# Cross-attention: two heads' row maxima turned by one transposition and carried to the queries' rows by SyncE's queue

## The chip, the cores and the metric

The kernel runs on one core of one Trainium2 chip. The metric is the device time of one execution in microseconds (us), as the median of several runs. The core's engines are TensorE (PE in the profile, with PEld for its weight loads), VectorE (DVE), ScalarE (ACT), GpSimd (POOL) and SyncE (SP), which here only issues transfers (DMAs). Each works through its own instruction stream in order, and they meet at semaphores.

## The reference

A decoder layer on `x` (16 x 224 x 512, float32): causal self-attention with rotary positions, cross-attention over a context of 750 positions, and a mixture-of-experts feed-forward part, each behind a layer norm and with a residual. The change lies in the cross-attention:

```python
q = (x @ Wq).reshape(B, N, HEADS, hd).transpose(0, 2, 1, 3)         # B 16, N 224, HEADS 16, hd 32
k = (context @ Wk).reshape(B, M, HEADS, hd).transpose(0, 2, 1, 3)   # M 750
v = (context @ Wv).reshape(B, M, HEADS, hd).transpose(0, 2, 1, 3)
scores = jnp.einsum('bhid,bhjd->bhij', q, k) * scale
scores = jnp.where(context_mask[:, None, None, :], scores, max_neg)
attn = jax.nn.softmax(scores, axis=-1)
out = jnp.einsum('bhij,bhjd->bhid', attn, v)
out = out.transpose(0, 2, 1, 3).reshape(B, N, DIM)
return out @ Wo
```

## The kernel before

The three parts of the layer run one after the other; the cross-attention is the function `cross_attention`. It loops over 16 batches `b`, and in each over four groups `g` of four heads `j`. With `t = 4 * b + g` a group is numbered through the whole stage. Batches 2 to 14 are iterations of a hardware loop; the first two and the last are written out.

**Scores twice.** For each head TensorE first forms the scores with the queries as rows (`scores`, two halves `h` of 112 queries), and VectorE takes their row maximum (`maximum`) into `mx`, 112 queries on partitions, [head, half] along the free side. One group later TensorE forms them again with the keys as rows (`shifted`, three units of 2 x 125 keys), this time with the maximum already taken off, so that ScalarE can go straight to the exponential (`exps`). For that the operands are stacked. `q_st` holds per head 32 rows of high parts, 32 again, 32 of low parts, then row 96 (ones) and rows 97 and 98: the negated maximum of each query, split into a high and a low part. `k_st` holds the keys' parts in its first 96 rows, the mask in row 96 and ones in rows 97 and 98. `scores` uses rows 0 to 96, `shifted` rows 0 to 98.

**How the maximum gets there.** `turn_max(u, t, i)` handles two heads (`i` = 0: heads 0 and 1, `i` = 1: heads 2 and 3). For each of their four columns of `mx` (two heads, two halves) it transposes the column, broadcast to 128 columns, so that the maxima of 112 queries stand along the free side of every partition of a PSUM bank `pj`. `high_max` on ScalarE writes rows 96 to 98 of `q_st` from the same rows of that bank, and `low_max` on VectorE corrects them with a per-row factor `less`, so that row 96 is 1, row 97 the high and row 98 the low part. TensorE waits for `low_max` (`done(...)`, the semaphore `pj_free`) before the first `shifted` of these heads.

**The order.** All engines follow a schedule written by hand. For each head of a group TensorE's stream holds `scores` of half 0, `shifted` of the same head of the group before (two units), `first_gap`, the third unit, `scores` of half 1 and `second_gap`; after four heads come the `values` of the group before. The gaps hold the projections of coming keys, queries and values, each into one of three banks `pj`, taken in turn and named by `UNITS`. Two kinds of these units are maximum turns. `M0_g` (`i` = 0 of group g) is turned in the first gap of head 3 and needed at head 0 of the next group. `M1_g` (`i` = 1 of the group before g) is turned in the second gap of head 0 of group g and needed at head 2 of the same group.

**SyncE's queue** issues all transfers in one order: `place_k` (copies of the projected key parts into four slots of `k_st`, 3 or 4 transfers a head, 16 for groups 0 and 1, 12 for groups 2 and 3), `place_q` (12 transfers for half of the heads), the loads of context and mask (`load_ctx`), of `x` and of the residual, and the stores. `place_k` waits until both halves of the keys are split (units `K..0`, `K..1`, VectorE's `low_k`) and, per head, until `shifted` is through with the slot.

Of the kernel before, what the change touches and what calls it, by code (L numbers as in the profile page):

```python
# [6 lines left out]
F32 = mybir.dt.float32  # L7
# [9 lines left out]
P = 128  # L17
# [807 lines left out]
def cross_attention(nc, x1, x1n, ctx, cmask, w_o, router_w, cst, x2, rows_w, logits, op):  # L825

    with ExitStack() as outer:
# [9 lines left out]
        with ExitStack() as c:  # L837
# [11 lines left out]
            mx = sb(c, "x_mx", [HT, 4, 2])  # L849
            less = sb(c, "x_less", [P, 1])  # L850
            pt = [op.pt[0], sb(c, "x_pt1", [KR, 3, 2 * T]), op.pt[2], op.pt[3]]
# [10 lines left out]

            gate, filled, zeroed, stored, rw_turned, rw_out, wo_loaded = (
                sem("x_" + n) for n in ("gate", "filled", "zeroed", "stored", "rw_turned", "rw_out", "wo_loaded"))
            x_loaded, c_loaded, m_loaded, xres_loaded = op.x_loaded, op.c_loaded, op.m_loaded, op.xres_loaded
# [24 lines left out]
            def k_mult(g):  # L890

                return 16 * (4 if g < 2 else 3)

            def placed(b, g):
# [11 lines left out]
            with nc.Block() as block:  # L906
                @block.sync
                def _(sp):
# [29 lines left out]
                    def place_k(t, b, g, units):  # L938
# [5 lines left out]
                        if below(t, 1):  # L944
                            sp.wait_ge(zeroed, 1)
                        for j in range(4):
# [12 lines left out]
                    def place_q(b, half, units):  # L959
# [5 lines left out]
                        for j in range(4):  # L965
                            rows = slice(32 * j, 32 * j + 32)
                            for s, p in enumerate((0, 0, 1)):
                                sp.dma_start(q_st[32 * s:32 * s + 32, 8 * half + j:8 * half + 8:4, :].bitcast(F32),
                                             qT[p][rows, 2 * half:2 * half + 2, :].bitcast(F32)).then_inc(q_placed[half], 16)

                    load_x(1, unit_of(-1, "X1"))
                    sp.dma_start(wo[:], w_o.rearrange("(k p) n -> p k n", p=P)).then_inc(wo_loaded, 16)
# [5 lines left out]
                    def body(b, first, last, more):  # L978
                        t = 4 * b
                        if not last:  # L980
                            load_ctx(b + 1)
                        place_k(t + 1, b, 1, [unit_of(b, "K10"), unit_of(b, "K11")])
                        place_q(b, 1, [unit_of(b, "Q2"), unit_of(b, "Q3")])
                        if not below(b, 2):
                            load_res(b - 1)
                            store_rows(b - 2)
                        place_k(t + 2, b, 2, [unit_of(b, "K20"), unit_of(b, "K21")])
                        if more:
                            load_x(b + 2, unit_of(b, "X1"))
                        place_k(t + 3, b, 3, [unit_of(b, "K30"), unit_of(b, "K31")])  # L990
                        if not first:
                            store(b - 1, unit_of(b, "O1"))
                        if not last:
                            place_q(b + 1, 0, [unit_of(b, "Q0"), unit_of(b, "Q1")])
                        if not last:
                            place_k(t + 4, b + 1, 0, [unit_of(b, "K00"), unit_of(b, "K01")])

                    body(0, True, False, True)
# [16 lines left out]
                def _(pool):  # L1015

                    fills = [(ones[:], 1.0), (less[:], -1.0), (less[96:97, :], 0.0)]
                    fills += [(k[96:99, :].bitcast(F32), 1.0) for k in k_st]
                    for n, (f, value) in enumerate(fills):
                        pool.memset(f, value).then_inc(filled, 1)  # L1020
                        pool.wait_ge(filled, n + 1)
                    pool.nop().then_inc(zeroed, 1)

# [45 lines left out]
                def _(pe):  # L1069
# [143 lines left out]
                    pe.wait_ge(rw_out, 1)  # L1213
                    pe.wait_ge(zeroed, 1)
                    pe.wait_ge(wo_loaded, 16)

                    def body(b, first, last):
# [79 lines left out]
                        for g in range(4):  # L1297
# [3 lines left out]
                            for j in range(4):  # L1301
                                pe.wait_ge(k_placed[j], placed(b, g))
                                scores(n, g, j, 0)
                                if prev:
                                    if j == 0:
                                        done(U(f"M0_{gp}") if g else unit_of(b - 1, "M0_3"))
                                    elif j == 2:
                                        done(U(f"M1_{g}"))
                                    shifted(n - 1, gp, j, (0, 1))
                                first_gap(g, j)  # L1310
                                if prev:
                                    shifted(n - 1, gp, j, (2,))
                                scores(n, g, j, 1)
                                second_gap(g, j)
# [13 lines left out]
                    n, last = 4 * B, lambda name: unit_of(B - 1, name)  # L1328
                    done(last("M0_3"))
                    shifted(n - 1, 3, 0, range(3))  # L1330
                    turn_max(last("M1_4"), n - 1, 1)
# [4 lines left out]
                    done(last("M1_4"))  # L1336
                    shifted(n - 1, 3, 2, range(3))
# [18 lines left out]
                def _(act):  # L1356
# [104 lines left out]
                    def body(b, first, last):  # L1461
# [6 lines left out]
                        def first_gap(g, j):  # L1468
# [13 lines left out]
                            elif j == 3:  # L1482
                                high_max(U(f"M0_{g}"), g, 0)
                                if g == 0 and not last:
                                    high_x(U("X0"), 0)
                                elif g == 1 and old:
                                    out_rows(U("N1"), 1)
                                elif g == 2 and not last:
                                    high_ctx(U("C01"), 0, 1)

                        def second_gap(g, j):
                            gp, prev = (g + 3) % 4, not (first and g == 0)
                            if j == 0:
# [7 lines left out]
                                if prev:  # L1501
                                    high_max(U(f"M1_{g}"), gp, 1)
                            elif j == 1:
# [50 lines left out]
                    n = 4 * B  # L1554
                    exps(n - 1, 0, range(3))
                    high_max(unit_of(B - 1, "M1_4"), 3, 1)
                    for j in range(1, 4):
                        exps(n - 1, j, range(3))
# [8 lines left out]
                def _(dve):  # L1567
# [97 lines left out]
                    def body(b, first, last):  # L1665
# [6 lines left out]
                        def first_gap(g, j):  # L1672
                            n, prev, pprev, gp = t + g, not (first and g == 0), not (first and g < 2), (g + 3) % 4
                            if j == 0:
# [4 lines left out]
                            elif j == 1:  # L1679
                                if prev:  # L1680
                                    low_max(U(f"M1_{g}"), 2 * n, gp, 1)
                            elif j == 2:
                                if pprev:
                                    invert(n - 2, 0)
                            else:
# [4 lines left out]
                                if g == 2 and not last:  # L1690
                                    low_ctx(b, 2, 0)
                                low_max(U(f"M0_{g}"), 2 * n + 1, g, 0)

# [67 lines left out]

                    n = 4 * B
                    root(RLN_STEPS * (B - 1))
# [4 lines left out]
                    low_max(unit_of(B - 1, "M1_4"), 2 * n, 3, 1)  # L1768
                    dve.wait_ge(exp_done, 3 * 4 * n)
# [728 lines left out]
```

## Time and profile before

| | |
|---|---|
| median of 3 runs | 3782.72 us (3779.25 to 3786.2) |
| span of the profiled execution (first to last instruction) | 3781.0 us |
| TensorE busy | 3636.5 us, 96% |
| VectorE busy | 2363.4 us, 63% |
| ScalarE busy | 1731.8 us, 46% |
| GpSimd busy | 1298.8 us, 34% |
| maximum turns (512 transpositions), busy | 71.1 us |

The span is what the profile gives as the time of its execution; the runs' median is 1.7 us above it. The cross-attention takes from about 1075 to 2470 us of the span. The durations of TensorE's matmuls overlap, since they are pipelined: how long a part of its stream takes is read from one start to the next, not from the durations.

### The profile page before, as it was taken

The numbers are of one execution on the slowest core, as the hardware profiler recorded it, in microseconds if no ns is written. First come the engines' busy times: TensorE is split into PE (matmuls) and PEld (weight loads), VectorE is DVE, ScalarE is ACT, GpSimd is POOL, SyncE is SP. The second block draws the span as 40 slices with busy tenths as digits, with TensorE's granted clock in tenths as the row PEclk, the third lists the DMA queues.
The fourth block names the chain that finished last, engine by engine and source line by source line (L and its number), as shares of the span: only waits on it lengthen the run. The fifth ranks groups of instructions, "written<-read, shape, count | busy, mean of one in ns | idle before, by whom it ended". The sixth has DMA issues, their size and how long they took to land. (4 is left out here: it accounts for less than half of the span.)

```text
span 3781.0 us, 84211 instructions
## 1 busy us (share of the span) xinstructions
PE 3636.5 (96%) x28244; PEld 3136.9 (83%) x28244; DVE 2363.4 (63%) x5547; ACT 1731.8 (46%) x4277; POOL 1298.8 (34%) x1385
## 2 busy tenths in 40 slices
PE   7999999999979999999999999849999999999999
PEld 6888888888868888888888888639999899989998
DVE  6788888888856666666666666576434434334343
ACT  4555555555535555555555555413333333333332
POOL 1333333333316556666556566510101101011010
PEclk9999999999979999999999999869999999999999
DMA  4222222222243343444434443223424334243232
GB/s 125 59 54 63 54 63 54 63 54 63 50 138 100 104 111 105 107 116 107 123 96 111 106 107 97 66 69 93 123 84 123 101 99 123 84 121 121 86 108 69
DMA packets 315057, 349.72 MB, mean 92 GB/s; under 512 B 45308, under 2 KB 232036, under 8 KB 314884
## 3 DMA queue, kind: packets, MB, share of 16 engines
q1 hardware_dynamic: 305796, 318.26, 30.7%
q0 software_dynamic: 9088, 29.17, 2.5%
q8 instruction: 106, 1.74, 0.2%
q14 instruction: 67, 0.55, 0.0%
HBM read 183.23 MB, written 38.91 MB: 59 GB/s over the span
## 5 line engine op out<-in xcount | busy, mean ns | idle before, releaser
L1605 DVE TENSOR_REDUCE x_mx<-x_psS 112x1 f32<-112x752 f32 x512 | 479.8, 937 | 380.1 <-PE x_psS L1158 376.7
L2401 DVE TENSOR_TENSOR hid<-e_psU,act_g 128x280 f32<-128x280 f32 x256 | 115.2, 450 | 626.1 <-PE e_psU L34 616.0
L1440 ACT ACTIVATE x_pt<-x_psE 125x448 f32<-125x448 f32 x768 | 389.5, 542 | 231.3 <-PE x_psE L1170 221.9
L1029 POOL TENSOR_TENSOR part<-x_pt 125x448 f32<-125x448 f32 x255 | 291.7, 1144 | 507.3 <-ACT x_pt L1440 498.5
L2027 POOL DMA_INDIRECT out<-ex_y,sidx x40 | 39.8, 994 | 1014.7 <-DVE ex_y L2435 1007.0
L611 POOL TENSOR_TENSOR qks<-qks,cos 128x448 f32<-128x448 f32 x128 | 147.6, 1153 | 677.7 <-DMA qks<-qk 677.7
L1158 PE MATMUL x_psS<-k_st,q_st 97*112 97x376 f32 x1024 | 287.4, 362 | 23.4 <-DMA k_st<-mk 15.5
L32 PE MATMUL e_psG<-ex_hi,g_hi 128*128 128x280 f32 x1024 | 303.8, 297 | 4.3 <-DVE ex_lo L2394 2.2
L32 PE MATMUL pj<-xT_hi,win_hi 128*128 128x224 f32 x1024 | 302.8, 296 | 1.4 <-DVE xT_lo L651 1.3
L1031 POOL TENSOR_TENSOR part<-part,x_pt 125x448 f32<-125x448 f32 x255 | 291.8, 1144 | 20.0
L32 PE MATMUL e_psU<-ex_hi,u_hi 128*128 128x280 f32 x1024 | 298.1, 291 | 0.3 <-DVE hid L2401 0.3
L34 PE MATMUL e_psG<-ex_hi,g_lo 128*128 128x280 f32 x1024 | 298.3, 291 | 0.0
L2186 ACT ACTIVATE act_g<-e_psG 128x280 f32<-128x280 f32 x256 | 103.7, 405 | 423.6 <-PE e_psG L34 417.0
L34 PE MATMUL e_psU<-ex_hi,u_lo 128*128 128x280 f32 x1024 | 297.6, 291 | 0.0
L33 PE MATMUL e_psG<-ex_lo,g_hi 128*128 128x280 f32 x1024 | 297.0, 290 | 0.0
L33 PE MATMUL e_psU<-ex_lo,u_hi 128*128 128x280 f32 x1024 | 297.0, 290 | 0.0
L34 PE MATMUL pj<-xT_hi,win_lo 128*128 128x224 f32 x1024 | 282.3, 276 | 0.0
L33 PE MATMUL pj<-xT_lo,win_hi 128*128 128x224 f32 x1024 | 281.6, 275 | 0.0
L1170 PE MATMUL x_psE<-q_st,k_st 99*125 99x224 f32 x1536 | 262.9, 280 | 6.4 <-ACT x_pt L1440 4.1
L1170 PEld LDWEIGHTS x_psE<-q_st,k_st 99*125 99x125 f32 x1536 | 236.0, 190 | 15.8 <-ACT x_pt L1440 11.3
L2190 ACT ACTIVATE hid_hi<-hid 128x280 fp32r<-128x280 f32 (+1 forms) x256 | 107.1, 419 | 288.3 <-DVE hid L2401 288.3
L674 DVE CUSTOM_DVE_ANT_0 pr<-psS,mask 112x112 f32<-112x112 f32 (+1 forms) x512 | 139.4, 329 | 128.1 <-issue 67.5
(301 smaller groups left out, 10880.3 us busy)
## 6 DMA issues: line engine op xcount, KB each, us to landing
k_st<-kT SPq DMA_DIRECT2D x768, 93.8 KB, 2.2
raw_g<-in_L_ffn_wg SPq DMA_DIRECT2D x128, 256.0 KB, 2.8
raw_u<-in_L_ffn_wu SPq DMA_DIRECT2D x128, 256.0 KB, 2.8
raw_d<-in_L_ffn_wd SPq DMA_DIRECT2D x128, 256.0 KB, 3.0
qks<-qk SPq DMA_DIRECT2D x512, 56.0 KB, 2.0
q_st<-qT SPq DMA_DIRECT2D x384, 56.0 KB, 2.0
ctxt<-in_ctx SPq DMA_DIRECT2D x16, 1125.0 KB
xt<-in_x SPq DMA_DIRECT2D x16, 448.0 KB, 3.7
```

The lines of the kernel that those rows point to most:

```text
L32: pe.matmul(out, lh, rh, start=first, stop=False)
L33: pe.matmul(out, lh, rl, start=False, stop=False)
L34: return pe.matmul(out, ll, rh, start=False, stop=last)
L611: pool.tensor_tensor(qks[i][:], qks[i][:], cos[:].unsqueeze(1).to_broadcast((P, 2, T)), ALU.mult)
L674: m = dve.tensor_tensor_reduce(pr[par][:, hd, to:to + n], psS[hd][0:HT, to:to + n], mask[:, h, 0:n], -SD ** -0.5, -NEG, ALU.add, ALU.min, ...
L1029: pool.tensor_tensor(part[:], pt[j][:, 0, :], pt[j][:, 1, :], ALU.add).then_inc(parted, 1)
L1031: pool.tensor_tensor(part[:], part[:], pt[j][:, 2, :], ALU.add).then_inc(parted, 1)
L1158: m = pe.matmul(psS[0:HT, s, 0:376], q_st[0:97, head, h * HT:(h + 1) * HT], k_st[4 * (g % 2) + j][0:97, SHALF[s]], start=True, stop=True)
L1170: m = pe.matmul(psE[(j + i) % 2][0:KR, s * T:(s + 1) * T], k_st[4 * (g % 2) + j][0:99, r * KR:(r + 1) * KR], q_st[0:99, 4 * g + j, :], sta ...
L1440: act.activation(pt[j][:, i, :], psE[(j + i) % 2][0:KR, 0:2 * T], ACT.Exp, scale=XD ** -0.5).then_inc(exp_done, 1)
L1605: dve.tensor_reduce(mx[:, j, h:h + 1], psS[0:HT, :, 0:376], AX.XY, ALU.max).then_inc(s_taken, 1)
L2401: dve.tensor_tensor(h[ring][:, halves[s]], psU[:, 0:CH], act_g[i][:, halves[s]], ALU.mult).then_inc(S["mul"], 1)
```

## The change

`turn_max` makes one transposition of the four columns together: `mx[:, 2i:2i+2, :]` is a weight of four columns, and the maxima come out on four partitions of the bank, 112 queries along the free side. ScalarE writes the negated high parts to `m_row[:, 0, :]`, VectorE the low parts to `m_row[:, 1, :]` (4 x 112 each). `place_max` on SyncE's queue then copies `m_row[:, 0, :]` to row 97 and `m_row[:, 1, :]` to row 98 of `q_st` for the two heads, two transfers that count up a new semaphore `m_placed`. TensorE waits for that semaphore, and ScalarE, before it overwrites `m_row`, for the copies before. Eight calls of `place_max` a batch stand in SyncE's order between the others. Row 96 of `q_st` is written once ahead of the stage and stays.

```diff
-            less = sb(c, "x_less", [P, 1])
+            m_row = sb(c, "m_row", [4, 2, HT], F32R)
...
+            def max_placed(t, i):
+
+                return 64 * t + 32 * i + 32
+
+            fills = [ones[:]] + [k[96:99, :].bitcast(F32) for k in k_st]
...
+                    def place_max(u, g, i):
+
+                        hold(sp, gate, pj_free[u.bank], u.after)
+                        head = 4 * g + 2 * i
+                        for r in range(2):
+                            sp.dma_start(q_st[97 + r:98 + r, head:head + 2, :].rearrange("p j (h t) -> p (j h) t", h=2).bitcast(F32),
+                                         m_row[:, r, :].bitcast(F32)).then_inc(m_placed, 16)
+
...
                         if not last:
                             load_ctx(b + 1)
+                        if not first:
+                            place_max(unit_of(b, "M1_0"), 3, 1)
                         place_k(t + 1, b, 1, [unit_of(b, "K10"), unit_of(b, "K11")])
+                        place_max(unit_of(b, "M0_0"), 0, 0)
                         place_q(b, 1, [unit_of(b, "Q2"), unit_of(b, "Q3")])
                         if not below(b, 2):
                             load_res(b - 1)
                             store_rows(b - 2)
+                        place_max(unit_of(b, "M1_1"), 0, 1)
                         place_k(t + 2, b, 2, [unit_of(b, "K20"), unit_of(b, "K21")])
+                        place_max(unit_of(b, "M0_1"), 1, 0)
                         if more:
                             load_x(b + 2, unit_of(b, "X1"))
+                        place_max(unit_of(b, "M1_2"), 1, 1)
                         place_k(t + 3, b, 3, [unit_of(b, "K30"), unit_of(b, "K31")])
+                        place_max(unit_of(b, "M0_2"), 2, 0)
                         if not first:
                             store(b - 1, unit_of(b, "O1"))
                         if not last:
                             place_q(b + 1, 0, [unit_of(b, "Q0"), unit_of(b, "Q1")])
+                        place_max(unit_of(b, "M1_3"), 2, 1)
                         if not last:
                             place_k(t + 4, b + 1, 0, [unit_of(b, "K00"), unit_of(b, "K01")])
+                        place_max(unit_of(b, "M0_3"), 3, 0)
...
+                    place_max(unit_of(B - 1, "M1_4"), 3, 1)
...
-                    fills = [(ones[:], 1.0), (less[:], -1.0), (less[96:97, :], 0.0)]
-                    fills += [(k[96:99, :].bitcast(F32), 1.0) for k in k_st]
...
                         pe.wait_ge(s_taken, 8 * t + 4 * i + 4)
                         o = bank(u)
-                        for n in range(4):
-                            m = pe.transpose(o[:, n * HT:(n + 1) * HT], mx[:, 2 * i + n // 2, n % 2:n % 2 + 1].to_broadcast((HT, P)),
-                                             ident[0:HT, 0:HT])
-                        m.then_inc(pj_full, 1)
+                        pe.transpose(o[0:4, 0:HT], mx[:, 2 * i:2 * i + 2, :].rearrange("p j h -> p (j h)"),
+                                     ident[0:HT, 0:HT]).then_inc(pj_full, 1)
...
                                 if prev:
-                                    if j == 0:
-                                        done(U(f"M0_{gp}") if g else unit_of(b - 1, "M0_3"))
-                                    elif j == 2:
-                                        done(U(f"M1_{g}"))
+                                    if j in (0, 2):
+                                        pe.wait_ge(m_placed, max_placed(n - 1, j // 2))
                                     shifted(n - 1, gp, j, (0, 1))
...
-                    def high_max(u, g, i):
-
+                    def high_max(u, t, i):
+
+                        if i or not below(t, 1):
+                            act.wait_ge(m_placed, max_placed(t, i) - 32)
                         o = full(u)
-                        act.activation(q_st[96:99, 4 * g + 2 * i:4 * g + 2 * i + 2, :],
-                                       o[96:99, 0:2 * T].rearrange("p (j t) -> p j t", j=2), ACT.Identity,
-                                       bias=ident[96:99, 96:97], scale=ident[96:99, 98:99]).then_inc(m_high, 1)
+                        act.activation(m_row[:, 0, :], o[0:4, 0:HT], ACT.Copy, scale=-1.0).then_inc(m_high, 1)
...
-                    def low_max(u, n, g, i):
+                    def low_max(u, n):
 
                         dve.wait_ge(m_high, n)
-                        rows = q_st[96:99, 4 * g + 2 * i:4 * g + 2 * i + 2, :]
-                        dve.scalar_tensor_tensor(rows, pj[u.bank][96:99, 0:2 * T].rearrange("p (j t) -> p j t", j=2),
-                                                 less[96:99, 0:1], rows.bitcast(F32), ALU.mult, ALU.add).then_inc(pj_free[u.bank], 1)
+                        dve.scalar_tensor_tensor(m_row[:, 1, :], pj[u.bank][0:4, 0:HT], -1.0, m_row[:, 0, :].bitcast(F32),
+                                                 ALU.mult, ALU.subtract).then_inc(pj_free[u.bank], 1)
```

Behind the last batch the turn of its heads 2 and 3 (`M1_4`) moves ahead of the last `shifted` of head 0, and ScalarE's and VectorE's halves of it move with it.

## Rows read from the trace of the kernel before

**Rows 1.** The page: busy time of the engines, share of the span, instructions.

```profile
PE 3636.5 (96%) x28244; PEld 3136.9 (83%) x28244; DVE 2363.4 (63%) x5547; ACT 1731.8 (46%) x4277; POOL 1298.8 (34%) x1385
```

**Rows 2.** One batch by windows: stretch, us, busy (x instructions) of PE, PEld, DVE, ACT, POOL; clock; DMA.

```profile
1432.94:1516.23 83.29, 82.45 (x711) 69.50 (x711) 56.33 (x83) 47.66 (x96) 49.96 (x63) 1.00 0.41 109
```

**Rows 3.** The maximum's three operations by line: duration ns min/median/max, first and last start.

```profile
L1148 PE MATMUL x_pj<-ident,x_mx x512: 257/258/394, 1113.5 to 2434.1; 112*128 112x112 f32 x171
...
L1392 ACT ACTIVATE q_st<-x_pj,ident x128: 717/717/721, 1114.1 to 2434.5; 3x448 fp32r<-3x448 f32 x128
...
L1611 DVE SCALAR_TENSOR_TENSOR q_st<-x_pj,x_less,q_st x128: 692/693/695, 1115.0 to 2439.3; 3x448 fp32r<-3x448 f32 x128
```

**Rows 4.** TensorE's timeline in this batch (L1170 is `shifted`): start, us, instructions.

```profile
1442.22 0.60 PE L1170 MATMUL x_psE<-q_st,k_st 99*125 99x224 f32 x4
...
1446.41 0.55 PE L1148 MATMUL x_pj<-ident,x_mx 112*128 112x112 f32 x4
1446.79 0.55 PE L1082 MATMUL x_pj<-ident,x_xt 112*128 112x112 f32 x4
1447.11 0.46 PE L1170 MATMUL x_psE<-q_st,k_st 99*125 99x224 f32 x2
...
1451.26 0.59 PE L1170 MATMUL x_psE<-q_st,k_st 99*125 99x224 f32 x4
...
1460.24 0.60 PE L1170 MATMUL x_psE<-q_st,k_st 99*125 99x224 f32 x4
...
1516.23 0.59 PE L1170 MATMUL x_psE<-q_st,k_st 99*125 99x224 f32 x4
```

**Rows 5.** The timeline of SyncE's queue in this batch: start, us the issue takes, transfer.

```profile
1436.20 0.29 SPq L919 DMA_DIRECT2D ctxt<-in_ctx  x1
...
1441.82 0.54 SPq L953 DMA_DIRECT2D k_st<-kT  x1
...
1450.41 0.53 SPq L953 DMA_DIRECT2D k_st<-kT  x1
...
1453.47 7.71 SPq L968 DMA_DIRECT2D q_st<-qT  x12
...
1462.37 0.36 SPq L936 DMA_DIRECT2D expert_rows<-x_xr  x1
...
1507.45 0.56 SPq L953 DMA_DIRECT2D k_st<-kT  x1
...
1517.91 0.82 SPq L957 DMA_DIRECT2D k_st<-mk  x1
```

**Rows 6.** VectorE's timeline in this batch: second key half and maximum M0_3.

```profile
1506.51 0.55 DVE L1599 TENSOR_TENSOR kT<-x_pj,kT 128x376 fp32r<-128x376 f32 x1
...
1514.02 0.69 DVE L1611 SCALAR_TENSOR_TENSOR q_st<-x_pj,x_less,q_st 3x448 fp32r<-3x448 f32 x1 [0.93 <-ACT q_st L1392]
```

**Rows 7.** The page, DMA issues of the whole span: number, KB each, us to landing.

```profile
q_st<-qT SPq DMA_DIRECT2D x384, 56.0 KB, 2.0
```

**Rows 8.** DMA issues from 1436.00 to 1444.40 us, and (last row) from 1462.60 to 1464.60.

```profile
mk<-in_mask_BxS_bf SPq DMA_DIRECT2D x1, 93.8 KB, 12.9
k_st<-mk SPq DMA_DIRECT2D x1, 2.9 KB, 7.0
...
k_st<-kT SPq DMA_DIRECT2D x2, 93.8 KB, 3.6
```

**Rows 9.** Windows around three idle gaps of TensorE, columns as in rows 2.

```profile
1094.61:1100.26 5.65, 0.00 (x1) 0.04 (x1) 0.00 (x0) 0.38 (x1) 0.00 (x0) 0.91 0.38 92
1100.26:1106.01 5.75, 5.75 (x21) 5.72 (x22) 2.29 (x3) 0.48 (x1) 0.00 (x0) 0.50 0.49 115
...
1122.71:1126.49 3.78, 3.78 (x13) 3.77 (x14) 1.47 (x2) 0.98 (x2) 0.00 (x0) 0.50 0.35 93
...
2457.49:2461.67 4.18, 0.00 (x0) 0.00 (x0) 3.34 (x17) 1.00 (x2) 0.00 (x0) 0.93 0.36 110
2461.67:2467.00 5.33, 4.56 (x24) 4.25 (x24) 0.62 (x1) 0.54 (x1) 0.00 (x0) 0.50 0.29 89
```

More of the change, by code:

```diff
@@ L861, in cross_attention @@
             psY, psZ = psYZ[:, 0:T], psYZ[:, T:2 * T]
-            gate, filled, zeroed, stored, rw_turned, rw_out, wo_loaded = (
-                sem("x_" + n) for n in ("gate", "filled", "zeroed", "stored", "rw_turned", "rw_out", "wo_loaded"))
+            gate, filled, m_placed, stored, rw_turned, rw_out, wo_loaded = (
+                sem("x_" + n) for n in ("gate", "filled", "m_placed", "stored", "rw_turned", "rw_out", "wo_loaded"))
             x_loaded, c_loaded, m_loaded, xres_loaded = op.x_loaded, op.c_loaded, op.m_loaded, op.xres_loaded
@@ L944, in place_k @@
                         if below(t, 1):
-                            sp.wait_ge(zeroed, 1)
+                            sp.wait_ge(filled, len(fills))
                         for j in range(4):
@@ L1015, in _ @@
                 def _(pool):
-                    fills = [(ones[:], 1.0), (less[:], -1.0), (less[96:97, :], 0.0)]
-                    fills += [(k[96:99, :].bitcast(F32), 1.0) for k in k_st]
-                    for n, (f, value) in enumerate(fills):
-                        pool.memset(f, value).then_inc(filled, 1)
+                    for n, f in enumerate(fills):
+                        pool.memset(f, 1.0).then_inc(filled, 1)
                         pool.wait_ge(filled, n + 1)
-                    pool.nop().then_inc(zeroed, 1)
                     def sum_blocks(t, g, heads=range(4)):
@@ L1213, in _ @@
                     pe.wait_ge(rw_out, 1)
-                    pe.wait_ge(zeroed, 1)
+                    pe.wait_ge(filled, len(fills))
                     pe.wait_ge(wo_loaded, 16)
@@ L1328, in _ @@
                     n, last = 4 * B, lambda name: unit_of(B - 1, name)
-                    done(last("M0_3"))
+                    turn_max(last("M1_4"), n - 1, 1)
+                    pe.wait_ge(m_placed, max_placed(n - 1, 0))
                     shifted(n - 1, 3, 0, range(3))
-                    turn_max(last("M1_4"), n - 1, 1)
                     totals(n - 2, 2)
@@ L1335, in _ @@
                     turn_rows(last("N1_14"), B - 2, 1)
-                    done(last("M1_4"))
+                    pe.wait_ge(m_placed, max_placed(n - 1, 1))
                     shifted(n - 1, 3, 2, range(3))
@@ L1482, in first_gap @@
                             elif j == 3:
-                                high_max(U(f"M0_{g}"), g, 0)
+                                high_max(U(f"M0_{g}"), t + g, 0)
                                 if g == 0 and not last:
@@ L1491, in second_gap @@
                         def second_gap(g, j):
-                            gp, prev = (g + 3) % 4, not (first and g == 0)
+                            prev = not (first and g == 0)
                             if j == 0:
@@ L1501, in second_gap @@
                                 if prev:
-                                    high_max(U(f"M1_{g}"), gp, 1)
+                                    high_max(U(f"M1_{g}"), t + g - 1, 1)
                             elif j == 1:
@@ L1554, in _ @@
                     n = 4 * B
-                    exps(n - 1, 0, range(3))
-                    high_max(unit_of(B - 1, "M1_4"), 3, 1)
-                    for j in range(1, 4):
+                    high_max(unit_of(B - 1, "M1_4"), n - 1, 1)
+                    for j in range(4):
                         exps(n - 1, j, range(3))
@@ L1672, in first_gap @@
                         def first_gap(g, j):
-                            n, prev, pprev, gp = t + g, not (first and g == 0), not (first and g < 2), (g + 3) % 4
+                            n, prev, pprev = t + g, not (first and g == 0), not (first and g < 2)
                             if j == 0:
@@ L1680, in first_gap @@
                                 if prev:
-                                    low_max(U(f"M1_{g}"), 2 * n, gp, 1)
+                                    low_max(U(f"M1_{g}"), 2 * n)
                             elif j == 2:
@@ L1691, in first_gap @@
                                     low_ctx(b, 2, 0)
-                                low_max(U(f"M0_{g}"), 2 * n + 1, g, 0)
+                                low_max(U(f"M0_{g}"), 2 * n + 1)
                         def second_gap(g, j):
@@ L1762, in _ @@
                     n = 4 * B
+                    low_max(unit_of(B - 1, "M1_4"), 2 * n)
                     root(RLN_STEPS * (B - 1))
@@ L1767, in _ @@
                     out_y(n - 2, 2)
-                    low_max(unit_of(B - 1, "M1_4"), 2 * n, 3, 1)
                     dve.wait_ge(exp_done, 3 * 4 * n)
```

## Prediction

> **What bounds the kernel now.** I read the page's busy shares first [rows 1]: TensorE is busy for 96% of the span, the next engine for 63%. Then the busy time by stretches, for one batch of the cross-attention stage [rows 2]: TensorE works 82.45 of 83.29 us at its full clock (2.4 GHz), VectorE 56 and ScalarE 48. So in this stage what leaves TensorE's stream is won, and every wait that is put into it is lost. The rest of the kernel is not touched. Then the SyncE queue's own timeline, since the change gives that queue new work on the path between the maxima and the matmuls. It is no idle queue: it issues 16 key placements in 11.3 us (1507.45 to 1518.73) and 12 query placements in 7.7 us, in strict order [rows 5].
>
> All times below are in the batch of [rows 2]. "Need" is the time at which TensorE reaches the first shifted product of the heads in question, and s is how late TensorE runs against before.
>
> **What is saved.** A maximum turn is four transpositions. From the first to the next instruction of the stream they take 0.38 us [rows 4], in the rest of this batch 0.32 to 0.39. Three of four go: 0.27 us, 8 times per batch, 2.2 us. Over 16 batches that is 35 us, and it is all the change can win. ScalarE's copy (717 ns for 448 elements) and VectorE's difference (693 ns) [rows 3] shrink to 112 elements. No row has that shape; between nothing and what they cost now I take 0.3 us each. VectorE and ScalarE have slack, so this buys no time in itself, only about 0.8 us earlier values for the queue. Dropping three small fills at the start and writing a row less of `q_st` cost and win nothing that shows.
>
> **What is added.** Eight times per batch two transfers go from `m_row` to rows 97 and 98, and TensorE waits for both. An issue costs between 0.59 us (32 partitions) and 0.82 us plus a 0.18 us gap (one row of `mk`) [rows 5]; the new ones have four pieces, and I take 0.62 from start to start. Landing takes 2.0 us from the start of the issue [rows 7]. So a placement with a free queue needs 0.62 + 2.0 = 2.6 us after VectorE's value. The question at each of the eight places is when the queue comes free and how far away the need is.
>
> *Place A, M0_3, needed at 1516.23* [rows 4]. VectorE ends at 1514.71 [rows 6]; even a free queue would land the value after the need. But the queue is not free: `place_max` stands behind `place_k` for the next group, which starts after the second half of the keys is split (1506.51 + 0.55 [rows 6]) and issues until 1518.73. The two issues start at 1518.8 and 1519.4 and land at 1521.4. The need comes at 1516.23 - 0.27 = 1516.0. Wait: 5.4 us. It repeats at full size in each batch, since the keys' placement is itself released by work of TensorE that has shifted with it.
>
> *Place B, M1_0 and M0_0, needed at 1442.22 and 1451.26* [rows 4]. With A behind it, s = 5.4 - 0.27 = 5.1. The context load, issued at 1436.20 [rows 5], moves to about 1437.4 behind the two new issues. What the profile shows in its shadow: the `mk` row issued at 1443.67 landed only 7.0 us later, 14.5 us after the context's issue, and the mask 12.9 us after its own [rows 8]. M1_0 is issued at about 1444 and so lands at about 1451.4, where TensorE wants it at 1442.22 + 4.9 = 1447.2: 4.2 us, s = 9.2. The Trainium skill (DMA: Bandwidth & Descriptors, Queues, rings and completion order) says that each DMA engine takes its descriptors in ring order; the 7.0 us against 2.0 us agree with that. If the small transfers slipped past the context load instead, B would cost 5.0 in all, as worked out under the lower bound.
>
> Meanwhile the keys of group 1 start at 1441.82 + 4.9. The fourth head's (1450.41 + 4.9 = 1455.3) overwrite a slot that the late stream still reads: its last read ended at 1447.57 [rows 4], now 9.2 later, 1456.8: 1.5 us more. M0_0 takes the turn that the queries had at 1453.47: 1453.47 + 4.9 + 1.5 = 1459.9, the second at 1460.5, landed at 1462.5. The need is 1451.26 + 9.2 - 0.27 = 1460.2. Wait 2.3, s = 11.2. B in sum: 6.5 us.
>
> *Place C, M1_1, needed at 1460.24* [rows 4]. Behind M0_0 the queue issues 12 queries, a load and a store of 448 KB (until 1462.73 before [rows 5], now 7.7 later, 1470.4), then M1_1 at 1470.5 and 1471.1. Transfers behind those two landed in 3.6 us [rows 8] against 2.0; I take 3.0: 1474.1. The need is 1460.24 + 11.2 - 0.27 = 1471.2. Wait 2.9.
>
> *The other four.* For M0_1 VectorE is done at 1467.9 and the need is at 1473.9, for M1_2 1482.5 and 1486.6: no wait. M0_2 (1494.3 and 1497.7) has some 0.6 us to spare, M1_3 about nothing; I cost them at 0, and a dearer issue would show there next. What stands behind the new waits: in TensorE's strict stream everything, and with it exps, maxima and the key slots; on SyncE the queries for groups 2 and 3 have over 10 us to spare.
>
> Per batch: 5.4 + 6.5 + 2.9 - 2.2 = 12.6 us. A full batch occurs 15 times (the last has no keys to place for a next one). The first batch has no M1_0, and already waits for keys at its first boundary; I estimate 4 us for it. 15 x 12.6 + 4 = 193 us.
>
> **The clock.** TensorE has hardly any idle stretch in this stage now. Where one of 5.65 us occurs, near its start, the clock falls to 1.2 GHz and stays there for 5.75 us of work after it; after one of 4.18 us it was low for at least 5.33 us [rows 9]. At half clock 5.75 us of work are 2.9 us lost; another gap, of 7 us, was followed by 3.8 us at half clock, 1.9 us lost; the mean is 2.4. Wait A is of that length. Of its 2.4 us about half is absorbed, since M1_0's landing hangs on the context and not on TensorE. One of the later waits may drop the clock too, with half a chance. I take 2.0 us per batch, 30 us. The Trainium skill (TensorE: Matmul & The Clock Gate, Why this matters for your kernels) warns that waits between bursts of matmuls cost the full clock; the gaps of 5.65 and 4.18 us agree. [...]
>
> **Sum.** 3781.0 + 193 + 30 = 4004 us of span. The runs' median is 1.7 us above the profiled span, so 4006.
>
> **Bounds.** Low: small transfers pass the large ones and the clock costs nothing. Then B is only M0_0: 1453.47 + 4.9 + 0.62 + 2.0 = 1461.0 against 1456.0, 5.0 us; C lands at 1471.5 against 1469.7, 1.8 us; 5.4 + 5.0 + 1.8 - 2.2 = 10.0 per batch, 155 in sum, 3938. High: each issue takes 1.0 us (1.8 us more per batch) and two clock drops count in full (4.8): 19.2 per batch, 4075.
>
> **The rivals.**
> - *Hidden transfers, faster.* If the queue were free at A, B and C within 2.6 us of each need, or nearly, only the saving stands: 3783 - 35 = 3748. For it: at four of eight places the value is ready early enough in the timeline of before. Against it: at A the needed value would leave the queue at 1518.8 even with no cost at all, 2.8 us after the need. It decides if the waits stay under 2.2 us per batch; A alone is more. 5%; within 0.2% of before, where the two cancel, 3%.
> - *Only A counts.* The stream, once late, finds later placements ready. Then 15 x 5.4 - 35 = 46, 3829. Against it: M0_0's queue work is released by the second half of the keys, which is as late as TensorE is. Cases between this and the low bound: 18%.
> - *More than the high bound*: M0_2 and M1_3 wait too, clock low through whole groups. 9%.
> - *My forecast*, waits at A, B and C with one clock drop or so: 65%, its own range 3938 to 4075.
>
> **How the numbers follow.** The range reaches down into the partial case, to 3880, and up to 4080. About 0.2% is what a measurement of this kernel can tell from no change. Faster 5%, same 3%, slower 92%.
>
> **What the profile after would show.** Idle time of TensorE before the shifted products (line of `shifted`), released by DMAs into `q_st`: 5.4 us at the first head of group 0, 4 us at its third, 2 us at the first and 3 us at the third head of group 1, none in groups 2 and 3. A batch of 96 to 99 us. Turns: one transposition, 128 in all. Keys' issues still 11.3 us per 16. A clock under 1.0 after A. It would be wrong if the new issues took 0.3 us, if M1_0 landed in 2 us beside the context load, or if the queue's holds let later groups drift until the waits meet at one place.

## The result, and the profile after

The changed kernel takes 4020.0 us (median of 5 runs, 4015.4 to 4020.6) against 3782.7 us: the ratio is 1.062, with a 95% interval of 1.061 to 1.063. That is slower, within the predicted range and 14 us above the predicted 4006 us. The single terms came out less well than their sum, as the following rows show. Of the runs below, one of experiment 3's four took 4284 us at a granted clock of 0.82, where the other three had 0.95, and is left out of its median.

One batch of the stage by windows: stretch, us, busy (x instructions) of PE, PEld, DVE, ACT and POOL, granted clock, DMA share, GB/s. The first row is a whole batch, the others are the three long waits and the work behind each; the first of these waits ends where the batch begins, and the batch closes with one like it, of 4.82 us.

```profile
1582.98:1681.95 98.97, 86.76 (x686) 71.70 (x687) 52.06 (x82) 43.10 (x96) 50.02 (x62) 0.93 0.36 92
1578.12:1582.98 4.86, 0.00 (x1) 0.00 (x1) 0.94 (x1) 0.00 (x0) 0.04 (x1) 0.71 0.27 61
1582.98:1586.97 3.99, 3.98 (x14) 3.99 (x15) 0.00 (x0) 0.98 (x2) 0.00 (x0) 0.50 0.26 81
1604.12:1607.35 3.23, 0.00 (x0) 0.01 (x1) 1.47 (x2) 0.11 (x1) 1.65 (x2) 1.00 0.17 41
1607.35:1610.86 3.51, 3.51 (x13) 3.51 (x14) 0.00 (x0) 0.98 (x2) 0.00 (x0) 0.51 0.33 82
1618.00:1620.25 2.25, 0.00 (x1) 0.01 (x1) 1.71 (x2) 0.83 (x2) 1.39 (x2) 1.00 0.83 257
1620.25:1624.52 4.27, 4.27 (x22) 4.26 (x23) 0.81 (x1) 1.91 (x4) 0.82 (x1) 0.60 0.45 106
```

A batch takes 98.97 us where it took 83.3 [rows 2]. TensorE is idle for 12.2 us of it, and it is busy for 86.8 us although it has less to do: behind each of the three long waits it works at 1.2 GHz for 4.0, 3.5 and 3.4 us (in the last row, at 0.60 over 4.27 us, that is 3.4 us at half clock).

TensorE's timeline in the same batch (L1189 is `shifted`, L1168 the turn, L1177 `scores`); in brackets the idle time before the instruction and what ended it.

```profile
1582.98 0.75 PE L1189 MATMUL x_psE<-q_st,k_st 99*125 99x224 f32 x2 [4.86 <-DMA q_st<-m_row]
...
1588.49 0.26 PE L1168 MATMUL x_pj<-ident,x_mx 112*4 112x112 f32 x1
1588.64 0.60 PE L1177 MATMUL x_psS<-k_st,q_st 97*112 97x376 f32 x2
...
1594.88 0.69 PE L1189 MATMUL x_psE<-q_st,k_st 99*125 99x224 f32 x4 [0.69 <-DMA q_st<-m_row]
...
1607.35 0.90 PE L1189 MATMUL x_psE<-q_st,k_st 99*125 99x224 f32 x3 [3.23 <-DMA q_st<-m_row]
...
1620.25 0.69 PE L1189 MATMUL x_psE<-q_st,k_st 99*125 99x224 f32 x4 [2.25 <-DMA q_st<-m_row]
```

These are the four needs of [rows 4]: M0_3 (place A, which closes the batch there and opens it here), M1_0 and M0_0 (place B), M1_1 (place C). A fifth or sixth wait does not occur; the other four placements are in time. The turn's one transposition holds the stream for 0.15 us here, and for 0.10 to 0.13 us at five other places of the batch.

SyncE's queue in this batch; the second number of `x2` rows covers both transfers of a placement.

```profile
1580.52 1.28 SPq L982 DMA_DIRECT2D q_st<-m_row  x2
1582.56 0.29 SPq L925 DMA_DIRECT2D ctxt<-in_ctx  x1
1590.48 1.24 SPq L982 DMA_DIRECT2D q_st<-m_row  x2
1604.89 1.28 SPq L982 DMA_DIRECT2D q_st<-m_row  x2
1616.04 1.44 SPq L982 DMA_DIRECT2D q_st<-m_row  x2
```

An issue takes 0.62 us (the median of all 256). The forecast had taken that for the time from start to start, which is 0.67 to 0.75 us here. TensorE goes on 1.75 us after the start of the second issue at A (1581.23) and at M0_0 (1605.60). It is 3.7 us at M1_0, behind the context load, and 3.5 us at M1_1, behind two transfers of 448 KB.

### The profile page after: what moved, and what is told of

Its sections match the earlier page's. It is cut to its first block and busy times, and to the rows that moved or that the text cites. A ratio compares the mean times of both kernels' runs of the same rounds, so it can differ in the third digit from the quotient of the medians.

```text
span 4018.7 us, 84035 instructions
## 1 busy us (share of the span) xinstructions
PE 3703.0 (92%) x27860; PEld 3168.8 (79%) x27860; DVE 2294.3 (57%) x5547; ACT 1658.1 (41%) x4277; POOL 1298.0 (32%) x1383
## 5 line engine op out<-in xcount | busy, mean ns | idle before, releaser
L1189 PE MATMUL x_psE<-q_st,k_st 99*125 99x224 f32 x1536 | 287.0, 299 | 175.5 <-DMA q_st<-m_row 165.8
L1189 PEld LDWEIGHTS x_psE<-q_st,k_st 99*125 99x125 f32 x1536 | 250.0, 205 | 208.4 <-issue 160.4
L1177 PE MATMUL x_psS<-k_st,q_st 97*112 97x376 f32 x1024 | 294.0, 369 | 21.3 <-DMA k_st<-mk 12.9
```

Source lines behind the costliest of these rows:

```text
L1177: m = pe.matmul(psS[0:HT, s, 0:376], q_st[0:97, head, h * HT:(h + 1) * HT], k_st[4 * (g % 2) + j][0:97, SHALF[s]], start=True, stop=True)
L1189: m = pe.matmul(psE[(j + i) % 2][0:KR, s * T:(s + 1) * T], k_st[4 * (g % 2) + j][0:99, r * KR:(r + 1) * KR], q_st[0:99, 4 * g + j, :], sta ...
```

## The experiments

All were timed beside the kernel before, which had medians of 3780.6 to 3781.2 us in these comparisons.

**1. No placement.** What do the turn and the split win by themselves? ScalarE's wait for the copies goes as well.

```diff
                     def place_max(u, g, i):
-                        hold(sp, gate, pj_free[u.bank], u.after)
...
+                        return
...
-                                    if j in (0, 2):
-                                        pe.wait_ge(m_placed, max_placed(n - 1, j // 2))
+                                    if j == 0:
+                                        done(U(f"M0_{gp}") if g else unit_of(b - 1, "M0_3"))
+                                    elif j == 2:
+                                        done(U(f"M1_{g}"))
...
-                        if i or not below(t, 1):
-                            act.wait_ge(m_placed, max_placed(t, i) - 32)
```

> The changed kernel without place_max: rows 97 and 98 of q_st keep their ones, so the maxima are computed, turned and split but never taken off (this part of the computation is left out). TensorE waits for the split as the kernel before does. My theory (the placements on SyncE's queue cost everything, the rest is a gain): only the saving of three of four transpositions is left, 128 x 0.27 = 35 us, so 3748 us, granted clock of the cross-attention 1.0 as before. Rival (the small operations on four partitions, or the changed order, cost time themselves): 3783 us or more.

Measured: 3768.8 us, ratio 0.9964 (0.9951 to 0.9976). So the placements, with the waits for them, cost all of the 251 us between this kernel and the changed one, but the gain against the kernel before is 12.5 us and not 35. A batch by windows:

```profile
1517.80:1600.30 82.50, 80.92 (x688) 67.08 (x687) 52.04 (x83) 42.61 (x96) 49.99 (x62) 1.00 0.42 110
```

TensorE's work fell by 1.5 us against [rows 2], the batch by 0.8: its idle time rose from 0.8 to 1.6 us.

**2. One transposition of four, in the kernel before.** Is it TensorE's shorter stream that gives too little, or something in the new copies?

```diff
-                        for n in range(4):
+                        for n in range(1):
                             m = pe.transpose(o[:, n * HT:(n + 1) * HT], mx[:, 2 * i + n // 2, n % 2:n % 2 + 1].to_broadcast((HT, P)),
```

> The kernel before with one of the four transpositions of each turn; the other three columns of the maxima are left as they lie in the bank (left out: the maxima of three of four columns). Everything else, the order and the way into q_st too, is that of before. Theory (the stream of TensorE is shorter by 3 x 0.07 us at 8 places, 1.7 us per batch, but it meets VectorE and ScalarE earlier and gives some back): 3765 to 3770 us, as the run without placements. Rival (the shorter copies on ScalarE and VectorE, which this kernel has not, matter too): 3775 us or more; or all of it is won: 3755 us.

Measured: 3772.9 us, ratio 0.9981 (0.9971 to 0.9990). The gain of 8 us is what TensorE's saving alone brings. The time lies between the theory's band (missed by 3 us) and the rival's 3775. The two intervals just overlap, so whether the smaller copies bring the other 4 to 5 us is not settled.

**3. Only place A early.** `place_k` and `place_q` get an argument that names a placement to issue behind one head's transfers.

```diff
-                    def place_k(t, b, g, units):
+                    def place_k(t, b, g, units, between=None):
...
+                            if between is not None and j == between[0]:
+                                place_max(*between[1:])
...
-                            place_k(t + 4, b + 1, 0, [unit_of(b, "K00"), unit_of(b, "K01")])
-                        place_max(unit_of(b, "M0_3"), 3, 0)
+                            place_k(t + 4, b + 1, 0, [unit_of(b, "K00"), unit_of(b, "K01")],
+                                    (1, unit_of(b, "M0_3"), 3, 0))
+                        else:
+                            place_max(unit_of(b, "M0_3"), 3, 0)
```

> Only place A is changed: the placement of M0_3 is issued behind the second head's keys of place_k, not behind the fourth. My theory (A waits for the queue's 16 key transfers): its wait of 4.9 us goes to under 0.7, and with it the 4.0 us at half clock behind it (2.0 us lost). The placement M0_0 stays where it was, released by VectorE's second key half, so the later waits stay: 15 x (4.9 - 0.5 + 2.0) = 96 us less than 4020, 3924 us. Rival (the queue as a whole is the limit, a wait only moves on to the next place): the later waits grow by what A loses, 4000 to 4020 us.

Measured: 4054.8 us (three runs, 4038.8 to 4060.9), ratio 1.070 (1.067 to 1.073), some 35 us slower than the changed kernel. Theory and rival were both wrong, my theory by 131 us. TensorE's and SyncE's timelines of one batch:

```profile
1611.75 0.54 PE L1195 MATMUL x_psE<-q_st,k_st 99*125 99x224 f32 x1 [9.79 <-DMA q_st<-m_row]
```

```profile
1597.95 0.29 SPq L925 DMA_DIRECT2D ctxt<-in_ctx  x1
1602.35 1.30 SPq L986 DMA_DIRECT2D q_st<-m_row  x2
```

The wait at A is gone, and M1_0's has grown from 0.7 to 9.8 us. M1_0 is issued at 1602.35 and lands 9.4 us later, 13.8 us after the context load was issued. It hangs on that load, and that load on SyncE's queue. TensorE was sent ahead into a wait whose end does not depend on it. M0_0 and M1_1 wait for 1.52 and 3.80 us in the same batch, so the waits sum to 15.1 us where they were 11.0, and the batch takes 102.5 us.

**4. All placements early, M1_0 ahead of the context load.** `M0_3` moves as in experiment 3, and `place_q` gets the same argument as `place_k`.

```diff
+                        if not first:
+                            place_max(unit_of(b, "M1_0"), 3, 1)
                         if not last:
                             load_ctx(b + 1)
-                        if not first:
-                            place_max(unit_of(b, "M1_0"), 3, 1)
-                        place_k(t + 1, b, 1, [unit_of(b, "K10"), unit_of(b, "K11")])
-                        place_max(unit_of(b, "M0_0"), 0, 0)
-                        place_q(b, 1, [unit_of(b, "Q2"), unit_of(b, "Q3")])
+                        place_k(t + 1, b, 1, [unit_of(b, "K10"), unit_of(b, "K11")], (1, unit_of(b, "M0_0"), 0, 0))
+                        place_q(b, 1, [unit_of(b, "Q2"), unit_of(b, "Q3")], (0, unit_of(b, "M1_1"), 0, 1))
...
-                        place_max(unit_of(b, "M1_1"), 0, 1)
-                        place_k(t + 2, b, 2, [unit_of(b, "K20"), unit_of(b, "K21")])
-                        place_max(unit_of(b, "M0_1"), 1, 0)
+                        place_k(t + 2, b, 2, [unit_of(b, "K20"), unit_of(b, "K21")], (1, unit_of(b, "M0_1"), 1, 0))
```

> All placements early: M0_3, M0_0 and M0_1 behind the second head's keys, M1_1 behind the first head's queries, M1_0 ahead of the context load. The number and kind of transfers are those of the changed kernel. My theory (only the turn in the queue costs): no wait for q_st above 0.7 us, clock 1.0, 3750 to 3770 us, faster than before. Rival (the trip through a transfer itself is too long for these places, 0.6 + 1.8 us at least, wherever it stands): waits of 1 us or more stay at several places and with them half-clock stretches, 3800 us or more.

Measured: 3875.1 us, ratio 1.026 (1.024 to 1.028). The placements' waits did go, to at most 0.5 us from 1260 to 2200 us of the span. But neither side had named the one that came in their place, at the first `scores` of group 1:

```profile
1567.67 0.60 PE L1180 MATMUL x_psS<-k_st,q_st 97*112 97x376 f32 x2 [4.43 <-DMA k_st<-mk]
```

That is the mask's row of the keys. Its first issue now stands 6.7 us behind the context load's, where it stood 12.8 us behind it in the changed kernel, and TensorE goes on 14.9 us after the load's issue (1552.78).

**5. The same order, but with the context load back ahead of M1_0.**

> The early placements of the run before, but with the context load back at its old turn, ahead of M1_0's placement. The last runs showed a wait that moved on to M1_0 (9.8 us a batch) once A was early. My theory now (M1_0 lands only when the context load, issued just ahead of it, is through): the waits at A, M0_0 and M1_1 go, one of about 10 us at M1_0 stays, with a half-clock stretch: 15 x (10 + 2.5) us above the 3769 us without placements, 3955 us. Rival (it was the late queue, not the context load, that held M1_0): under 3875 us, since no placement stands behind more than two heads' keys.

Measured: 3958.0 us, ratio 1.047 (1.045 to 1.048), 3 us from what was expected. The one long wait of a batch:

```profile
1581.63 0.75 PE L1192 MATMUL x_psE<-q_st,k_st 99*125 99x224 f32 x2 [9.86 <-DMA q_st<-m_row]
```

**6. The context load cut in two.** 125 partitions become 112 and 13; the first load, ahead of the stage, and the semaphore's counts follow.

```diff
-                        sp.dma_start(ctxt[:], at(cv, b, "o p k d -> (o p) k d")).then_inc(c_loaded, 16)
+                        for rows in (slice(0, 112), slice(112, KR)):
+                            sp.dma_start(ctxt[rows], at(cv, b, "o p k d -> (o p) k d")[rows]).then_inc(c_loaded, 16)
...
-                        pe.wait_ge(c_loaded, 16 * b + 16)
+                        pe.wait_ge(c_loaded, 32 * b + 32)
```

> The changed kernel, order untouched, only the context load is cut into two transfers, 112 and 13 partitions in place of 125. My theory (125 partitions leave the load to a few of the DMA engines, the same ones that the four pieces of a placement use; 112 spread it over all): the load takes 3 to 5 us in place of 13, M1_0 lands 2 us after its issue, its wait of 0.7 us and the hold of the later keys behind it go: 1 to 2 us per batch, 3990 to 4005 us. Rival (the load is bound elsewhere, as by the memory): 4020 us.

Measured: 4017.7 us, ratio 1.063 (1.061 to 1.064): no difference from the changed kernel. DMA issues around the context load, first of the changed kernel and then of this one: KB each, us to landing.

```profile
mk<-in_mask_BxS_bf SPq DMA_DIRECT2D x1, 93.8 KB, 11.4
```

```profile
mk<-in_mask_BxS_bf SPq DMA_DIRECT2D x1, 93.8 KB, 6.6
```

The load is faster: the mask behind it lands after 6.6 us, and the issue of that mask holds SyncE for 0.36 us in place of 3.86. M1_0's wait is gone. Yet M0_0's went from 3.23 to 4.16 us:

```profile
1608.06 1.01 PE L1191 MATMUL x_psE<-q_st,k_st 99*125 99x224 f32 x4 [4.16 <-DMA q_st<-m_row]
```

M0_0 stands behind the 16 key transfers, and these start when the second key half is split. From there (VectorE done at 1593.97) to TensorE's going on it is 14.1 us, the same as in the changed kernel (1593.23 to 1607.35). What was won ahead of M1_0's need was waited for at M0_0's.

The Trainium skill (DMA: Bandwidth & Descriptors, Why a DMA increments its semaphore by 16 and not by 1) says that a transfer is split over the largest number of engines, 16 at most, that divides its slowest dimensions. By this rule, as an estimate, 125 partitions go to 5 engines (0.31 of 16) and 112 to 16. The landing of 6.6 us against 11.4 agrees, and so does the mean busy share of the 16 DMA engines, here in tenths over 11 us in 40 slices, first of the changed kernel from 1582 us, then of this one from 1583 us:

```profile
DMA  0000022223223333333335456643333333333333
```

```profile
DMA  0000068597999999999999976200000000000000
```

**7. Filling matmuls inside the waits.** They keep TensorE at work where it waited, and write what `shifted` overwrites.

```diff
+FILL = {(0, 0): 40, (1, 0): 26, (1, 2): 18}
...
+                    def fill(t, j, count):
+
+                        pe.wait_ge(exp_done, 12 * t + 3 * j - 1)
+                        for i in range(count):
+                            pe.matmul(psE[j % 2][0:KR, 0:T], wq[0][:, 0, 0:KR], wq[1][:, 0, 0:T], start=True, stop=True)
...
+                                    if FILL.get((g, j)) and not below(b, 1):
+                                        fill(n - 1, j, FILL[g, j])
```

> The changed kernel with matmuls added that compute nothing of use, in TensorE's stream ahead of the three long waits: 40 at A, 26 ahead of M0_0's and 18 ahead of M1_1's wait, some 0.11 us each at full clock, so 4.4, 2.9 and 2.0 us inside waits of 4.9, 3.2 and 2.3 us. My theory (5.4 us per batch are lost to the half clock behind the waits): the clock stays full, the transfers land when they did, and 15 x 5.4 = 80 us go: 3940 us, though TensorE has more to do. Rival (the clock costs little, the batch is set by SyncE's queue): 4000 to 4020 us, or more by what the added matmuls overrun the waits.

Measured: 4015.7 us, ratio 1.062 (1.060 to 1.064), as the rival said. But its reason is only half of it. The rows show that the clock did stay full behind A, and that TensorE then ran into M1_0:

```profile
1596.97 1.17 PE L1192 MATMUL x_psE<-q_st,k_st 99*125 99x224 f32 x4 [3.29 <-DMA q_st<-m_row]
...
1622.97 0.70 PE L1192 MATMUL x_psE<-q_st,k_st 99*125 99x224 f32 x4 [0.66 <-DMA q_st<-m_row]
...
1683.11 0.70 PE L1192 MATMUL x_psE<-q_st,k_st 99*125 99x224 f32 x4 [0.37 <-DMA q_st<-m_row]
```

M1_0 was issued at 1589.97 and lands 13.0 us after the context load (1583.95). The new gap brought a half-clock stretch of its own, 5.9 us from 1596.97 on.

**8. The filling matmuls and the cut load together.**

> The filling matmuls in the waits (as in the run of 4016 us) together with the context load cut into 112 and 13 partitions (as in the run of 4018 us). Each alone gained nothing. My theory (the time at half clock behind A was hidden under the wait for the context load, so that neither shows without the other): the clock stays full, K11 comes 2.0 us earlier per batch and with it the keys and M0_0, and 1.5 us behind M1_1: 15 x 3.5 = 50 us, 3965 us. Rival (the half clock costs nothing in this batch, SyncE's queue sets it alone): 4015 us.

Measured: 3969.0 us, ratio 1.050 (1.048 to 1.052). Against the changed kernel's 4020.0 us each edit alone gained 2 to 4 us, which the runs hardly tell from nothing, and both together 51; 3965 us were expected. So the half clock does cost time, and in the changed kernel the part of it that lies between A and M1_0 was hidden under the context load. A batch:

```profile
1573.70:1668.90 95.20, 90.71 (x770) 76.35 (x770) 52.04 (x82) 42.96 (x96) 49.97 (x62) 1.00 0.39 96
```

**9. Only place A early, M1_0 ahead of the context load, and that load cut.**

> Only M0_3's placement early (behind the second head's keys), with M1_0 ahead of the context load and that load cut. The run with M0_3 early alone was slower than the changed kernel (4058 us), since M1_0 then waited 9.8 us. My theory (that wait was the context load's): with the load out of the way A's 4.8 us and the 2.0 us at half clock behind it go: 15 x 6.8 = 102 us below 4018, 3916 us, with the waits of M0_0 (4.2) and M1_1 (2.3) as they were. Rival (a wait that is removed is made up at the next place): 3990 us or more.

Measured: 3912.0 us, ratio 1.035 (1.033 to 1.036), 4 us from what was expected. The early placement at A, which cost 35 us in experiment 3, gains 106 us against experiment 6 once M1_0 no longer stands behind the context load (in experiment 6, with the load cut, M1_0 had no wait left to lose).

**10. All placements early and the load cut.**

> All placements early and M1_0 ahead of the context load, as in the run of 3875 us, and the context load cut into 112 and 13 partitions. In that run one wait was left, 4.4 us a batch for a row of the mask behind the context load. My theory (turn in the queue, and a context load on few DMA engines, are all that the placements cost): no wait above 0.7 us, clock 1.0, the level of the kernel without placements, 3765 to 3780 us, 0 to 0.5% faster than the kernel before. Rival (the trip of a transfer is too long for some place): 3790 us or more.

Measured: 3781.1 us, ratio 0.9999 (0.9990 to 1.0008). The waits of TensorE from 1260 to 2200 us of the span (us in total, times, longest), and one batch by windows:

```profile
PE x_psE L1194 <- DMA q_st<-m_row: 6.2, 15, 1.2
```

```profile
1607.30:1689.50 82.20, 80.60 (x685) 66.40 (x683) 51.48 (x83) 42.78 (x96) 49.58 (x60) 1.00 0.44 111
```

The same trip through a transfer costs 166 us of waits in the changed kernel's stage and 10 us here. The full expected gain isn't there: this is even with the kernel before. Batches can be compared from TensorE's start of one M0_0 need to the next. The 13 batches of the loop take 1079.5 us (1284.4 to 2363.9) against 1085.1 before, 0.4 us less each; without placements it was 1073.5. The first batch takes 3.0 us more than before (80.8 against 77.8), and the last, up to its last `shifted`, 3.9 us more (80.8 against 76.9), which takes that back. Of the 3.9 us, 2.3 us are there without any placement too (experiment 1, 79.2 us).

**11. The cut load alone, in the kernel before.**

> The kernel before, only with the context load cut into 112 and 13 partitions: what the cut is worth without any placement, so that the run beside it is not credited with it. The kernel before waits 15.5 us in all for mask rows, most of it in the first two batches behind context loads. Theory: 3 to 10 us of these go, 3773 to 3780 us. Rival: no difference, 3782 us.

Measured: 3774.5 us, ratio 0.9979 (0.9970 to 0.9989). This one beats both kernels, without any of the change: its waits of TensorE for the mask's rows are 7.0 us in all, where the kernel before has 15.5. It also means that experiment 10 has this gain in it: against it the change, with its placements at their best, is 0.2% behind.

## Why the prediction was right, point by point

*Direction and size.* They were right: 14.6 us per batch were forecast and 15.7 came. The mechanism was right too. Placements on SyncE's queue at A, M1_0, M0_0 and M1_1 come late and the other four do not; experiments 1, 9 and 10 show that their lateness is nearly all that the change costs (239 of 251 us go with early placements and the cut load), and that it is the turn in the queue, with the context load in it, and not the trip. But three terms were mis-sized: per batch the waits were put 3.8 us too high, the clock 3.4 us too low and the saving 1.4 us too high. They cancelled, and that the sum came within 14 us is luck.

*The waits*: forecast 14.8 us per batch (5.4, 4.2, 2.3, 2.9), measured 11.0 (4.86, 0.69, 3.23, 2.25). At A 0.25 us are the landing, 1.75 us in place of 2.0. M1_0's term is the one that failed: I had it landing 14.0 us after the context load's issue, and in the changed kernel it was 12.3 us. TensorE, slowed by the clock, also came 2 us later than the term assumed. M0_0 waited 0.9 us longer than forecast: its end hangs on the second key half, whose transfers start 1.4 us before TensorE goes on at M1_0 (1593.51 and 1594.88), where the forecast had 4.7. The 1.5 us that the fourth head's slot was to cost there did not occur: the 16 issues ran through in 11.2 us. At M1_1 the landing came later than assumed (3.5 us after the second issue, not 3.0), but TensorE, at half clock behind M0_0, came later still.

*The clock*: forecast 2.0 us per batch, measured about 5.4. Behind A, M0_0 and M1_1 there are 4.0, 3.5 and 3.4 us of work at half clock, half of which is lost. I had counted on one drop; there are three, since gaps of 3.23 and 2.25 us brought it about as well. Waits and clock are not independent: what TensorE loses behind A and M0_0 makes it come later to M1_0 and M1_1 and wait less there. Experiments 7 and 8 show this property of the term, which I had put at "about half is absorbed": loss behind A is hidden until the context load is shortened.

*The saving*: forecast 2.2 us per batch, measured 0.8 (experiment 1). I had taken 0.27 us at all eight places. At six of them one transposition holds the stream for 0.10 to 0.15 us where four held it for 0.32 to 0.38, 1.4 us together. At the other two nothing is won: behind M0_2's turn the next instruction starts after 0.36 us (0.39 before), behind M0_3's after 0.58 (0.57 before), where TensorE now waits 0.32 us for ScalarE's exponential. That wait and one of 0.4 us for a row of the mask are most of the 0.7 us by which the batch's idle time grew. The copies had been put at 0.3 us and measured 0.24 and 0.26.

*The sum*: 11.0 + 5.4 - 0.8 = 15.6 of the 15.7 us per batch, once each term is the measured one.

*The rivals.* "Hidden transfers" was priced at 3748. Experiment 10 made the transfers hidden and gave 3781, so even its condition would not have given that time. "Only A counts" rested on later placements being ready once TensorE is late; the changed kernel's own waits of 3.23 and 2.25 us speak against it, and experiment 6 shows the opposite for M0_0. "More than the high bound" needed waits at M0_2 and M1_3; there are none.

*Open.* Whether the smaller copies on ScalarE and VectorE are worth anything (experiments 1 and 2), and why the first batch and the last are longer in experiment 10; neither was tried further. How much the half clock costs in the changed kernel as it stands is open too, since experiment 7 brought a new half-clock stretch with it.

## What to carry to other kernels

A step moved to a DMA queue costs its turn in that queue before it costs its latency: list what the queue issues between the time when the value is ready and the need, and put the small urgent transfer between two heads' bulk transfers, not behind them. When a wait is removed, ask which clock the next one hangs on. If that is TensorE's own progress, the gain stays; if it is a queue or a large load, the wait moves on, and can grow. An edit that shows nothing alone may be one of two limits in a row, and only the pair tells.

## What was not expected of the hardware

- Idle gaps of 2.25 and 3.23 us, with full clock before them, were followed by 3.4 to 3.5 us at 1.2 GHz in the batch shown. So were the waits at the same two places in the other batches from 1406 to 2313 us of the changed kernel's span, at M1_1 down to 1.83 us. The waits of 1.46 to 1.57 us at M0_0 in experiment 3, and one of 2.18 us there (ending at 1317.01), were not. The shortest in [rows 9] had been 4.18 us.
- Cutting one load of 125 partitions into 112 and 13 shortened the landing of the mask behind it from 11.4 to 6.6 us, and the issue of that mask, which had held SyncE's queue for 3.86 us, to 0.36 us. By itself the cut made the kernel before 0.2% faster.
- A transfer from SBUF to SBUF of 1.8 KB was usable 1.75 us after its issue started, and took 0.62 us to issue, like the queries' transfers of 56 KB (0.60 us).
